# A sparse-expert kernel: the next expert's rows are turned by a block-swapping DMA and VectorE instead of TensorE

## The reference

```
scores = (tanh(xn @ gate_w.T) + 1) / 2
vals, idx = top_k(scores.T, 1024)                  # 8 experts, 1024 rows each
y = layernorm(xn[idx]) * gamma + beta              # (1024, 8, 512)
h = gelu(einsum('knd,nfd->knf', y, fc1s) + b1s)    # 2048 hidden
o = (einsum('knf,ndf->knd', h, fc2s) + b2s) * vals
out = xn.at[idx].add(o)
```

## Time and profile before

| | us |
|---|---|
| median of 3 runs | 2657.49 (2655.19 to 2657.57) |
| profiled execution | 2657.18 |
| its span | 2655.4 |
| TensorE busy | 2629.0 (99%) |
| VectorE busy | 2050.7 (77%) |
| ScalarE busy | 1498.4 (56%) |

### The profile page before, as it was taken

One profiled execution on the slowest core, in us unless ns is written; L12 is line 12 of the kernel. 1 busy time (PEld: TensorE's weight loads), 2 busy tenths in 40 slices (PEclk: granted clock), 3 DMA queues, 4 the chain that ended last, 5 costly groups with the idle time before them and its releaser, 6 DMA issues.

```text
span 2655.4 us, 39102 instructions
## 1 busy us (share of the span) xinstructions
PE 2629.0 (99%) x11816; PEld 2136.6 (80%) x11816; DVE 2050.7 (77%) x3514; ACT 1498.4 (56%) x2578; POOL 676.9 (25%) x1006
## 2 busy tenths in 40 slices
PE   8999999999999999999999999999999999999998
PEld 4588888888888888888888888888888888888886
DVE  8778888888888888788876768867788677786654
ACT  5744555555555565565545555665555655556553
POOL 5422222221222222223432214113141131321102
PEclk9999999999999999999999999999999999999999
DMA  9733222223333322235443425234253342533413
GB/s 365 261 127 111 80 94 87 90 93 111 111 112 111 111 73 83 92 95 161 151 133 110 116 67 145 80 96 131 64 142 85 93 132 67 136 91 88 100 56 72
DMA packets 139664, 300.28 MB, mean 113 GB/s; under 512 B 26224, under 2 KB 26352, under 8 KB 135664
## 3 DMA queue, kind: packets, MB, share of 16 engines
q1 hardware_dynamic: 105840, 201.54, 23.1%
q0 software_dynamic: 33664, 96.75, 14.8%
HBM read 244.46 MB, written 53.77 MB: 112 GB/s over the span
## 4 chain that ended last, share of the span: by engine, by line
PE 95%; DVE 1%; DMA 1%; issue 1%; ACT 1%; POOL 0%; SPq 0%; POOLq 0%; DVEq 0%; ACTq 0%
PE po L2530 9%; PE po L2532 9%; PE po L2531 9%; PE ring L1584 9%; PE ring L1585 8%; PE ring L1586 8%; PE pb L2530 4%; PE pb L2531 4%; PE pb L2532 4%; PE po L1622 4%; PE po L1623 4%; PE po L1624 4%; PE pc L2530 2%; PE pc L2531 2%; PE pc L2532 2%; PE pb L571 1%
## 5 line engine op out<-in xcount | busy, mean ns | idle before, releaser
L2530 PE MATMUL po<-w2h,hid_h 128*128 128x512 f32 x1024 | 402.1, 393 | 0.1
L1584 PE MATMUL ring<-xt_h,w_h 128*128 128x512 f32 x1024 | 400.1, 391 | 0.1
L2531 PE MATMUL po<-w2l,hid_h 128*128 128x512 f32 x1024 | 398.6, 389 | 0.0
L1585 PE MATMUL ring<-xt_l,w_h 128*128 128x512 f32 x1024 | 398.5, 389 | 0.0
L1586 PE MATMUL ring<-xt_h,w_l 128*128 128x512 f32 x1024 | 398.4, 389 | 0.0
L1373 DVE SCALAR_TENSOR_TENSOR u<-xin,cw,u 128x512 f32<-128x512 f32 x384 | 288.5, 751 | 75.8 <-issue 47.0
L2013 POOL DMA_INDIRECT out_dram<-res,idx_c x64 | 108.7, 1699 | 477.0 <-DVE res L2377 465.9
L1584 PEld LDWEIGHTS ring<-xt_h,w_h 128*128 128x128 f32 x1024 | 192.2, 188 | 40.9 <-DVE xt_l L542 0.9
L1586 PEld LDWEIGHTS ring<-xt_h,w_l 128*128 128x128 f32 x1024 | 192.2, 188 | 40.2
L2530 PEld LDWEIGHTS po<-w2h,hid_h 128*128 128x128 f32 x1024 | 192.3, 188 | 39.5 <-DVE hid_l L2367 0.5
L1585 PEld LDWEIGHTS ring<-xt_l,w_h 128*128 128x128 f32 x1024 | 192.3, 188 | 39.4
(11 more groups left out here) (300 smaller groups left out, 6307.5 us busy)
## 6 DMA issues: line engine op xcount, KB each, us to landing
w2r<-fc_in SPq DMA_DIRECT2D x256, 256.0 KB
wo<-wo_halves POOLq DMA_DIRECT2D x120, 512.0 KB, 4.5
w1r<-fc_in SPq DMA_DIRECT2D x144, 256.0 KB
x_tail<-x_in SPq DMA_DIRECT2D x64, 256.0 KB, 2.7
out_dram<-res SPq DMA_DIRECT2D x64, 256.0 KB, 2.0
g_x<-x_in SPq DMA_DIRECT2D x15, 1024.0 KB, 8.3
xt_rows<-g_xnt SPq DMA_DIRECT2D x15, 1024.0 KB, 9.9
rows<-xt_rows SPq DMA_DIRECT2D x15, 1024.0 KB, 6.2
```

The costliest lines, as they stand in the source:

```text
L1584: pe.matmul(ring[r % 2][:, :], w_h[:, r, q], xt_h[:, k, :], start=(k == 0), stop=False)
L1585: pe.matmul(ring[r % 2][:, :], w_h[:, r, q], xt_l[:, k, :], start=False, stop=False)
L2530: pe.matmul(dst, ah, bh, start=start, stop=False, skip_group_check=more)
L2531: pe.matmul(dst, ah, bl, start=False, stop=False, skip_group_check=more)
```

## The change

`t_bank` and its calls go, and with them the two bank tables. After the rows of a tile are normalised, SyncE stores the tile to a DRAM scratch (`rows_out`) and loads it back (`rows_back`), four loads per tile, one for each group of 32 partitions q. Partition 32q + p then holds, for each k (128 features) and each t (32 tokens), the 32 values of token 32t + p and features 128k + 32q onward: 32x32 blocks are swapped, the inside of a block isn't turned. A run in DRAM is 32 values. VectorE's block transpose (`t_turn`) then turns 16 blocks of 32x32 along a [128, 512] slice. B12 is turned into T1's tile, T3 is made before T1, and the lows wait for the last sum that reads their whole value (`LAST_SUM`). In the first expert the store and load of tile 0 come at SyncE's steps 16 and 18, of tile 1 at 21 and 22; later both stores come in pair 5 and the loads in pair 6. GpSimd's next gather waits for the last turn instead of the last bank.

```diff
+        def rows_out(e, i):
+            sp.wait_ge(c_nm, J * (2 * e + i + 1) + 1)
+            sp.dma_start(z_rows[i].rearrange("(j p) d -> p j d", p=P), rows[i][:, :, :]).then_inc(c_rows_out, 16)
+
+        def rows_back(e, i, out):
+            sp.wait_ge(c_rows_out, XT_STORED + 16 * out)
+            blocks = z_rows[i].rearrange("(t p) (k q c) -> q p k t c", p=QUAD, q=P // QUAD, c=QUAD)
+            for q in range(P // QUAD):
+                sp.dma_start(rows[i][q * QUAD:(q + 1) * QUAD, :, :].rearrange("p k (t c) -> p k t c", c=QUAD),
+                             blocks[q]).then_inc(c_rows_back, 16)
...
+            if n == FT:
+                rows_out(1, 0)
+            if n == FT + 2:
+                rows_back(1, 0, 1)
+            if n == FT + J + 1:
+                rows_out(1, 1)
+            if n == FT + J + 2:
+                rows_back(1, 1, 2)
...
+                if q == 5 and not last:
+                    for i in range(2):
+                        rows_out(e + 1, i)
+                if q == 6 and not last:
+                    for i in range(2):
+                        rows_back(e + 1, i, 2 * e + 2)
...
-                bank = R3 if name == "B21" else R1
-                act.wait_ge(c_t, bank_at(e, k, name) + 1)
-                act.copy(tw[name][k], bank[:, :]).then_inc(c_th, 1)
-                act.copy(th[name][k], bank[:, :]).then_inc(c_th, 1)
+                act.wait_ge(c_t, turned_at(e, k, name) + 1)
             else:
                 act.wait_ge(c_tr, sum_at(e, k, name) + 1)
-                act.copy(th[name][k], tw[name][k]).then_inc(c_th, 1)
+            act.copy(th[name][k], tw[name][k]).then_inc(c_th, 1)
...
-        def t_sum(e, k, name, free):
+        def t_turn(e, k, name, free):
+            i = 0 if name[2] == "1" else 1
             dve.wait_ge(c_p1, free + 1)
-            if name == "T1":
-                dve.wait_ge(c_t, bank_at(e, k, "B12") + 1)
-                dve.wait_ge(c_th, high_at(e, k, "whole B11") + 1)
-                dve.tensor_tensor(tw["T1"][k], R3[:, :], tw["B11"][k], ALU.subtract).then_inc(c_tr, 1)
-            elif name == "T3":
-                dve.wait_ge(c_th, high_at(e, k, "whole B22") + 1)
-                dve.tensor_tensor(tw["T3"][k], tw["B22"][k], R3[:, :], ALU.subtract).then_inc(c_tr, 1)
+            dve.wait_ge(c_rows_back, XT_STORED + 128 * e)
+            dve.transpose(tw["T1" if name == "B12" else name][k],
+                          rows[i][:, k if name[1] == "1" else 2 + k, :]).then_inc(c_t, 1)
+
+        def t_sum(e, k, name):
+            if name == "T3":
+                dve.wait_ge(c_t, turned_at(e, k, "B22") + 1)
+                dve.tensor_tensor(tw["T3"][k], tw["B22"][k], tw["T1"][k], ALU.subtract).then_inc(c_tr, 1)
+            elif name == "T1":
+                dve.wait_ge(c_tr, sum_at(e, k, "T3") + 1)
+                dve.tensor_tensor(tw["T1"][k], tw["T1"][k], tw["B11"][k], ALU.subtract).then_inc(c_tr, 1)
             elif name == "T2":
                 dve.wait_ge(c_tr, sum_at(e, k, "T1") + 1)
                 dve.tensor_tensor(tw["T2"][k], tw["B22"][k], tw["T1"][k], ALU.subtract).then_inc(c_tr, 1)
             else:
-                dve.wait_ge(c_th, high_at(e, k, "whole B21") + 1)
+                dve.wait_ge(c_t, turned_at(e, k, "B21") + 1)
...
+            if name in LAST_SUM:
+                dve.wait_ge(c_tr, sum_at(e, k, LAST_SUM[name]) + 1)
...
-        def t_bank(e, k, name, first=False):
-            if name == "B11" and k == 0:
-                pe.wait_ge(c_nm, J * (2 * e + 2) + 1)
-                if first:
-                    pe.wait_ge(c_tl, 2 * KD + 1)
-                else:
-                    pe.wait_ge(c_add, adds(e - 1, PAIRS - 1, ADD_FIRST) + 1)
-            elif name == "B11":
-                pe.wait_ge(c_th, high_at(e, 0, "B22") + 1)
-            elif name == "B12" and k == 1:
-                pe.wait_ge(c_th, high_at(e, 0, "B21") + 1)
-            elif name == "B22":
-                pe.wait_ge(c_th, high_at(e, k, "B11") + 1)
-            elif name == "B21":
-                pe.wait_ge(c_tr, sum_at(e, k, "T3") + 1)
-            turned(R1 if name in ("B11", "B22") else R3, 0 if name[2] == "1" else 1, k if name[1] == "1" else 2 + k)
...
-                for k, name in () if last else T_BANK_AT.get(x, ()):
-                    t_bank(e + 1, k, name)
...
+LAST_SUM = {"B11": "T1", "B22": "T2", "T1": "T2", "B21": "T4", "T2": "T4"}
+T_HIGH_AT = {0: (), 1: ((0, "B11"), (0, "B22")), 2: ((0, "T3"),), 3: ((0, "T1"),), 4: ((0, "T2"), (0, "B21")), 5: ((0, "T4"),),
+             7: ((1, "B11"), (1, "B22")), 8: ((1, "T3"), (1, "T1")), 9: ((1, "T2"),), 10: ((1, "B21"),), 11: ((1, "T4"),)}
+T_LOW_AT = {0: ((0, "turn", "B11"), (0, "turn", "B12"), (0, "turn", "B22")),
+            1: ((0, "turn", "B21"), (0, "sum", "T3")),
+            2: ((0, "sum", "T1"), (0, "low", "B11")),
+            3: ((0, "sum", "T2"), (0, "low", "B22")),
+            4: ((0, "sum", "T4"), (0, "low", "T3")),
+            5: ((0, "low", "T1"), (1, "turn", "B11")),
+            6: ((1, "turn", "B12"), (1, "turn", "B22")),
+            7: ((1, "sum", "T3"), (1, "sum", "T1")),
+            8: ((1, "sum", "T2"), (0, "low", "T2")),
+            9: ((1, "turn", "B21"), (0, "low", "B21")),
+            10: ((1, "sum", "T4"), (0, "low", "T4")),
+            11: ((1, "low", "B11"), (1, "low", "B22")),
+            12: ((1, "low", "T3"),),
+            13: ((1, "low", "T1"),),
+            14: ((1, "low", "T2"), (1, "low", "B21")),
+            15: ((1, "low", "T4"),)}
...
+FIRST_LOW_AT = {6: ((0, "turn", "B11"), (0, "turn", "B12"), (0, "turn", "B22"), (0, "turn", "B21")),
+                7: ((0, "sum", "T3"), (0, "sum", "T1"), (0, "sum", "T2"), (0, "sum", "T4")),
+                8: ((0, "low", "B11"), (1, "turn", "B11"), (1, "turn", "B12"), (1, "turn", "B22")),
+                9: ((0, "low", "B22"), (0, "low", "T3"), (0, "low", "T1"), (1, "turn", "B21")),
+                10: ((0, "low", "T2"), (0, "low", "B21"), (0, "low", "T4"), (1, "sum", "T3"), (1, "sum", "T1")),
+                11: ((1, "low", "B11"), (1, "sum", "T2"), (1, "sum", "T4")),
+                12: ((1, "low", "B22"), (1, "low", "T3"), (1, "low", "T1")),
+                13: ((1, "low", "T2"), (1, "low", "B21"), (1, "low", "T4"))}
```

More of the change, by code:

```diff
@@ L1762 @@
 HALF = D // 2
[L1763 to L1766, removed]
+SUMS = ("T3", "T1", "T2", "T4")
+PARTS = ("B11", "B22", "T3", "T1", "T2", "B21", "T4")
+TURNS = ("B11", "B12", "B22", "B21")
+QUAD = 32
 P1, P2, P6, P5, P7, P4, P3 = range(1, 8)
@@ L1829, in stage_experts @@
     rows = [ew.rows, ew.rows1]
+    z_rows = [t["z_rows"][i] for i in range(2)]
     yt_h = [xt_h, ew.w1[:, 4:8, :]]
@@ L1846, in stage_experts @@
     c_tr = m.count("f_tr")
+    c_rows_out, c_rows_back = sums.c_xt_store[0], sums.c_xt_store[1]
+    XT_STORED = 16 * NB // 4 + 1
     c_wh = m.count("f_wh")
@@ L1888, in shared_ahead, with turned_at @@
         return 128 * e - 128 + (shared(0, 28 + x) if x < 4 else shared(0, 24 + x))
-    def bank_at(e, k, name):
-        return 8 * e + 4 * k + BANKS.index(name) + 1
+    def turned_at(e, k, name):
+        return 8 * e + 4 * k + TURNS.index(name) + 1
     def high_at(e, k, name):
-        return 20 * e - 12 + 10 * k + HIGHS.index(name) + 1
+        return 14 * e - 6 + 7 * k + PARTS.index(name) + 1
     def low_at(e, k, name):
-        return 14 * e - 6 + 7 * k + LOWS.index(name) + 1
+        return 14 * e - 6 + 7 * k + PARTS.index(name) + 1
     def sum_at(e, k, name):
@@ L2048, in expert @@
             if not last:
-                pool.wait_ge(c_t, bank_at(e, 1, "B21") + 1)
+                pool.wait_ge(c_t, turned_at(e, 1, "B21") + 1)
                 for i in range(2):
@@ L2320, in t_step @@
             k, what, name = step
-            if what == "sum":
-                t_sum(e, k, name, free)
+            if what == "turn":
+                t_turn(e, k, name, free)
+            elif what == "sum":
+                t_sum(e, k, name)
             else:
@@ L2663, in expert @@
                 pair(e, q)
-            if not last:
-                t_bank(e + 1, 0, "B11")
-                t_bank(e + 1, 0, "B12")
             last_shares(e, FT - 2, FT - 1)
@@ L2684, in tensor @@
                     trn(T_AT.index(s - 1))
-                if g == 1:
-                    for k, name in FIRST_BANK_AT.get(s, ()):
-                        t_bank(1, k, name, True)
             if g == 0:
@@ L2727, in build @@
+FIRST_HIGH_AT = {7: ((0, "B11"), (0, "B22")), 8: ((0, "T3"), (0, "T1")), 9: ((0, "T2"), (0, "B21"), (0, "T4")),
+                 10: ((1, "B11"), (1, "B22")), 11: ((1, "T3"), (1, "T1")), 12: ((1, "T2"), (1, "B21"), (1, "T4"))}
+FIRST_LOW_AT = {6: ((0, "turn", "B11"), (0, "turn", "B12"), (0, "turn", "B22"), (0, "turn", "B21")),
[7 rows of a table added]
 def build(nc, t):
@@ L2731, in build @@
     slots_d = nc.dram_tensor("slots", (E * HI, LO), U32, kind="Internal").ap()
```

(1 more changed line is left out.)

## The result

The changed kernel's median is 2635.9 us (2635.4 to 2637.4, 4 runs) against 2656.7 (2655.2 to 2657.6, 4 runs) for the kernel before: a ratio of 0.9923, 95% interval 0.9906 to 0.9940. The forecast was 2638. Its profiled execution took 2637.4 us with a span of 2635.5, against 2657.2 and 2655.4.

The account below looks back on a forecast made before the run. TensorE, busy for 99% of the span, was taken as the bound. Transposes removed, 25.3 us, less 6 x 0.9 of new waits gave 19.9 us: span 2635.5, forecast 2638 (chance 0.52); overall range 2631 to 2672.

Parts of the forecast that it names:

- What goes from TensorE: TensorE, expert stage: the transposes of the next expert's rows go, 3.6 us per expert, 25.3 us over seven experts.
- What VectorE gains: VectorE, stored-tile phase: eight turns of 0.65 us, 5.2 us per expert, so TensorE waits 0.9 us in next pair 0.
- Rival C: A VectorE turn is two passes, 1.2 us: net +1.7 us per expert, 2664 us; chance 0.12.
- Rival A: VectorE's 5.6 idle us in the stored-tile phase hide all the turns: 2632 us; chance 0.09.
- What the queues gain: DMA loads of the rows: 13.5 ns per 128-byte piece, 13.8 us, at the semaphore 2.8 us before the first turn.
- rival B: Eight loads end after VectorE's first turn wants them, each microsecond late lost in six experts: 2661 at 20 ns; chance 0.22.
- First expert: In the first expert, block loads land near VectorE's first turns: no loss, at most 2 us once.

## Why the prediction was right

- **What goes from TensorE**: 3.6 us an expert. Confirmed by the steps (2.6 net, 3.6 with the two new waits) and by the run with one transpose per bank (0.104 us a transpose; 224 of them are 23 us, where the steps around the banks give 25). Right.
- **What VectorE gains**: a turn of 0.65 us. It is 0.59 to 0.63 from start to start, 667 to 701 ns long: one pass. Rival C falls. The running of VectorE's sum to 1805.8 against TensorE's P2 at 1805.15 gave a wait of 0.9 us; it is 0.64 in this expert and 0.55 to 0.71 over the six. Of the 0.9, 0.2 were the semaphore: from the end of the low (1799.15) to TensorE's start (1799.21) it is 0.06. That VectorE sets it is shown by the doubled turns and by the reordered lows. Rival A, that VectorE hides all, falls too, by 0.64 us an expert.
- **What was missed**: the double bank ahead of the last shares covered another wait, TensorE's for the low of hidden tile 15, 0.38 us. The sum took the whole 0.89 us of that bank as gain. The two together make 1.0 us per expert where the prediction had 0.9, which is why the total came out: 25.3 - 6 x 1.0 = 19.3 against 19.9 said, with 19.9 measured between the spans and 20.8 between the medians. Part of this agreement is luck: a term too large by 0.3 us and one left out of 0.4. And 0.4 of the 19.9 us between the two spans lie ahead of anything that was changed: expert 0's last own transposes start at 1374.07 before and at 1373.69 after.
- **What the queues gain**: 13.5 ns a piece was put, 11.7 measured; landing 1764.5 against a need at 1767.3 was put, a margin of 2.8 us, and it is 4.3. Most of the 1.5 more is an earlier start: the first load is issued 18.9 us before the first turn, where 17.6 was put. On time, so rival B falls for this kernel. B's own price was too low. Loads that come later also take longer, beside the scatters (20.3 us in place of 14.6), and TensorE comes back at half clock. Moved by one pair they cost 82 us, where B's rule, a microsecond for each one late, gives 6 x 12.2 = 73 for the lateness of the expert shown.
- **The Trainium skill's 512-byte rule** ("DMA: Bandwidth & Descriptors", Specifications) puts the smallest transfer for line rate at 512 B. The trace agrees so far: 128-byte pieces from DRAM to SBUF moved at 175 GB/s, the 2 KB rows on their way out at 399. The price that the prediction drew from the rest of it for rival B, that a 128-byte piece costs as much as a 512-byte one, 34 ns by its straight line, is not borne out: a piece took 11.7 ns. No run has 512-byte pieces, so what one of them costs is not shown.
- **First expert**: one wait of 0.7 us of VectorE for the blocks, none of TensorE; nothing to 2 us was put.

## What to carry to other kernels

Where one engine is the bound and never waits, price what is removed from it by the distance between starts. Then ask what wait stood under it: part of a removed instruction may have been cover. Where a second engine becomes as full as the first in one phase, the order in which it makes things counts. Sort its work by first use at the consumer; only then did a local exchange on the first engine pay here. Transfers of many small pieces cost nothing here while nothing waited for them. Put them where no other heavy traffic runs, and with slack, as lateness cost more here than its own length.

## What the runs showed of the hardware

- A DMA of 2048 pieces of 128 B occupies SyncE for 1.5 us at its issue when others are queued before it (11.93 us for eight); a 256 KB load in 2 KB rows takes 0.33 (median of 256).
- Small pieces of 128 B from DRAM: 11.7 ns each on an engine with nothing beside them (175 GB/s). 2 MB of them took 20.3 us from issue to use in place of 14.6 when 1 MB of accumulating scatters ran beside them.
- TensorE's clock: with two starts 0.50 to 1.24 us apart in a full stream it stayed at the 2.4 GHz level. After a phase with three short waits and starts 3.3 us apart it ran some eight matmuls at the 1.2 GHz level, from 1.5 us after it had resumed; after 10.7 to 13.1 us without a start, 7 to 14.
- A 128x512 fp32 block transpose on VectorE takes as long as a two-input sum of that size; TensorE's fp32 transpose of 128x128 costs 0.10 to 0.12 us in a stream of matmuls, though its record is 272 ns long.
